# Message sums of the build stage moved from a VectorE addition to a ScalarE copy and an accumulating transfer

## The chip, the core and the metric

One core of one Trainium2 chip runs the whole program in one launch. The metric is the device time of the program in microseconds (us), lower is better. TensorE is written PE, VectorE DVE, ScalarE ACT, GpSimd POOL, and the queue of the sync engine SP, as in the profile.

## The reference, cut to what matters

Four graph layers run over the same 3125 nodes with 64 features and 103125 edges. The change lies in the first layer alone. It computes, for every edge (row, col), a similarity of the two transformed node vectors, and sums weighted vectors of the neighbours:

```python
Wh = h @ W + b
sim = sum(Wh[row] * Wh[col]) / max(|Wh[row]| * |Wh[col]|, EPS)
base = adj_v * softplus(deg_coeff[0] * deg_v + deg_coeff[1]) * (row != col)
prop_pos = segment_sum((base * relu(sim))[:, None] * Wh[col], row)
prop_neg = segment_sum((base * -relu(-sim))[:, None] * Wh[col], row)
out = scale * (coeff[0] * prop_pos + coeff[1] * prop_neg + coeff[2] * Wh)
```

## The kernel before

The nodes are cut into 25 blocks of 128 (`NB = 25`). The edges are sorted, and the stage `build` (L686 to L1244) turns them into dense blocks: for block b it makes the 128 by 3200 matrix of edge counts (`c_row`, bf16), of edge weights (`a_row`) and of gates (`g_row`). Counts and gates are stored to HBM for the later layers; the weights are used at once for the first layer. All five engines run their own program, tied by semaphores that count completed operations.

The work of one **step** (the function `step` of each engine, 24 of them, for blocks w = 1 to 24) is two things interleaved: the one-hot matmuls of block w, and the message passing of block v = w - 1.

- The one-hots: POOL doubles the edge fields of a quarter o of the slots (`double`, L780), DVE compares them with numbers and multiplies (`onehots`, L1008: the comparisons at L1018 and L1020, called "hi" and "soh" here, the product "mv" at L1024). PE multiplies them in 11 **lots** (`lot`, L1155); quarter 0 holds lots 0 to 2, quarter 1 lots 3 to 5, quarter 2 lots 6 to 8, quarter 3 lots 9 and 10. Lots use two pairs of PSUM banks in turn, so lot i waits until ACT has emptied lot i - 2. ACT empties a lot with three instructions (`evacuate`, L915, lines L927 twice and L931; lot 5 takes four).
- The messages: PE makes similarities of up to 1024 columns (`sims`, L1171), ACT takes their positive part (`positive`, L945, "pos"), DVE combines them ("sim", L1051). PE transposes the weights of four blocks into the one bank AT (`turn`, L1182), DVE multiplies them with the similarities ("y", L1062), PE multiplies y with the block's vectors (`propagate`, L1192, "prop"). There are seven chunks (turn, y and prop 0 to 6) and four groups g of them (sims, pos and sim 0 to 3; groups 0 to 2 have 1024 columns, group 3 has 128).
- The sums: for each group DVE adds the 128x512 result of two props to the tile `passed` in SBUF (`add`, L1070, the instruction at L1074; the fourth is 64x128). Props of groups 1 and 2 wait until the bank PR has been read by the add of the group before; turn 0 of the next block waits for the fourth add, which reads bank AT. The semaphore `added` counts the adds.

The order is written out by hand. PE and ACT both walk `ORDER` (L673), ACT acting only on its entries "sims" and "lot"; DVE walks `VORDER` (L677):

```python
ORDER = [("sims", 0), ("lot", 0), ("turn", 0), ("lot", 1), ("sims", 1), ("turn", 1), ("lot", 2), ("lot", 3), ("turn", 2),
         ("prop", 0), ("prop", 1), ("sims", 2), ("turn", 3), ("lot", 4), ("lot", 5), ("lot", 6), ("lot", 7), ("turn", 4),
         ("prop", 2), ("prop", 3), ("sims", 3), ("turn", 5), ("lot", 8), ("lot", 9), ("lot", 10), ("turn", 6), ("prop", 4),
         ("prop", 5), ("prop", 6)]
VORDER = [("sim", 0), ("y", 0), ("hi", 1), ("hot", 1), ("y", 1), ("sim", 1), ("y", 2), ("hi", 2), ("hot", 2), ("add", 0), ("y", 3),
          ("sim", 2), ("y", 4), ("hi", 3), ("hot", 3), ("add", 1), ("y", 5), ("hi", 0), ("sim", 3), ("y", 6),
          ("hot", 0), ("add", 2), ("add", 3)]
```

"hot" is soh and mv; index 0 of "hi" and "hot" belongs to the next block. POOL in a step copies two small weight tiles once the last prop of the block before is done (`weights`, L794, copies at L803 and L804), then doubles quarters 1, 2, 3 and quarter 0 of the next block. SP stores the gates of the block before in two pairs of transfers, after 4 and after 8 lots of the block have been emptied (`gated_out`, L875), and the counts when all are (`counts_out`, L870). ACT starts a step only once the stores from the tiles that it will overwrite have landed (`begin`, L935).

A second pass over the same code with a run-time index exists for graphs with nodes of very high degree. It does not run with these inputs.

Of the kernel before, what the change touches and what calls it, by code (L numbers as in the profile page):

```python
# [5 lines left out]
ALU = mybir.AluOpType  # L6
# [7 lines left out]
P = 128  # L14
N = 3125
F = 64
# [22 lines left out]
LOTS = [(o, a, min(a + LOT, OH[o][1])) for o in range(4) for a in range(OH[o][0], OH[o][1], LOT)]  # L39
HI = 26  # L40
SQ = 32
CHUNKS = [(a, min(4, NB - a)) for a in range(0, NB, 4)]
# [637 lines left out]


def rounds_of(eng, table):
    return eng.value_load(table[0:1, 0:1], min_val=1, max_val=-(-E // SLOTS) + 1)


def build(nc, k, table, st, st_dram, deg, rec_dram, whT, rn_row, cap, uD, coef, prop, c16_dram, c_dram, g_dram, prime_dram):  # L686
# [3 lines left out]
    with Mem(nc, "b") as l:  # L690
# [14 lines left out]
        begun = l.sb("begun", [P, 6])  # L705
        sim, scale = [l.sb(f"sim{i}", [P, 1024]) for i in range(2)], l.sb("scale", [P, 512])
        y = [l.sb(f"y{i}", [P, 1024]) for i in range(2)]
# [7 lines left out]
        s = {n: l.sem(n) for n in names.split()}  # L715
        s_win, s["further"] = k["win"], k["further"]
        s_stored = [l.sem(f"stored{i}") for i in range(2)]
# [39 lines left out]
        def _(pool):  # L757
# [48 lines left out]
            def add_out(r, b, par):  # L806
# [13 lines left out]
                pool.wait_ge(s["further"], done + 80)  # L820

            def first(r):
                weights(r, 0, 0)
                early = not again(r)
                double(r * NB, 0, 0)
                double(r * NB, 0, 1)
                if early:
                    gather(2, 5, 7)
                double(r * NB, 0, 2)
                if early:  # L830
                    gather(3, 7, 9)
                double(r * NB, 0, 3)
                if early:
                    gather(3, 9, 11)
                double(r * NB + 1, 1, 0)
                if early:
                    gather(4, 11, 13)
                    pool.wait_ge(s["rounded"], ROUNDED)

            def step(r, b, par):  # L840
                w = r * NB + b
                weights(r, b, par)
                if again(r):
                    add_out(r, b - 1, 1 - par)
                for o in range(1, 4):
                    double(w, b, o)
                if not (isinstance(b, int) and b == NB - 1):
                    double(w + 1, b + 1, 0)

            def widen():  # L850
# [46 lines left out]
        def _(act):  # L897
# [45 lines left out]
            def positive(v, g):  # L943
                act.wait_ge(s["sims"], NG * v + (NG + g + 1))
                nc.scalar.activation(side(pos, g), both(g), ACT.Relu, scale=coef[:, 0:1]).then_inc(s["pos"], 1)  # L945

            def first(r):
                w = r * NB
# [9 lines left out]
            def step(r, b, par):  # L958
                w = r * NB + b
                begin(r, w, b, par)  # L960
                for what, i in ORDER:
                    if what == "lot":
                        evacuate(r, w, par, i)
                    if what == "sims":
                        positive(w - 1, i)

            def end(r):
# [7 lines left out]
        def _(dve):  # L975
# [94 lines left out]
            def add(v, g):  # L1070
                m, n = (P, 512) if g < NG - 1 else (F, P)
                dve.wait_ge(s["propped"], NC * v + (2 * NC + 1 + min(2 * g + 2, NC)))
                part, bank = k["passed"][0:m, g, 0:n], PR if g < NG - 1 else AT
                nc.vector.tensor_tensor(part, part, ps[0:m, bank, 0:n], ALU.add).then_inc(s["added"], 1)  # L1074
# [783 lines left out]
def four_layers(nc, x, src, dst, edge_attr_16, edge_weight, edge_weight_n2, L0_gnn_W, L0_gnn_b, L0_gnn_deg_coeff,  # L1858
# [13 lines left out]
    with Mem(nc, "k") as top:  # L1872
# [5 lines left out]
        k["rows"], k["win"] = [top.sem(f"rows{g}") for g in range(len(GATES))], [top.sem(f"win{g}") for g in range(len(GROUPS))]  # L1878
        k["further"], k["starts"] = top.sem("further"), top.sem("starts")
        table = top.sb("table", [1, 2], I32)  # L1880
# [46 lines left out]
```

## Time and profile before

| | us |
|---|---|
| median of 3 runs | 1071.21 |
| lowest and highest run | 1067.58, 1077.04 |
| the profiled execution, its own time | 1065.46 |
| its span in the trace | 1063.8 |
| mean granted PE clock, share of full | 0.934 |

The stage `build` takes from about 99 us to about 706 us of the span; its 24 steps lie between 151 and 687 us. In the timeline a row is: start, duration, engine, line, operation, output tile <- input tiles, shapes, number of merged instructions, and in brackets how long the engine had been idle before it and who released it. Instructions of one engine overlap by about 0.1 us at their ends, so start-to-start distances are shorter than durations.

### The profile page before, as it was taken

The page shows a single profiled execution, that of the slowest core. Times are in us where ns is not written, and L with a number is a line of the kernel's source. Part 1 is how long each engine was busy: PE and PEld are TensorE (multiplying, and loading weights), DVE is VectorE, ACT ScalarE, POOL GpSimd, SP SyncE. Part 2 cuts the span into 40 slices and gives each one's busy share as a digit, 9 for nine tenths or more (in the row PEclk, how much of TensorE's full clock was granted, in tenths as well). Part 3 has the DMA queues.
Part 4 walks back from the last instruction along what each step waited for, and adds up shares of the span by engine and source line. Part 5 has one row for each costly group of instructions (what it writes and reads, how often), then busy time and mean ns, then how long its engine had stood idle before and what let it go on. Part 6 is the DMA issues. An engine that isn't in the chain of part 4 may idle for free. (4 is left out here: it accounts for less than half of the span.)

```text
span 1063.8 us, 33473 instructions
## 1 busy us (share of the span) xinstructions
PE 850.4 (80%) x14240; PEld 596.1 (56%) x14240; DVE 902.9 (85%) x1310; ACT 583.1 (55%) x1994; POOL 170.9 (16%) x316
## 2 busy tenths in 40 slices
PE   0596558877888878887878888755999998999997
PEld 0362435544455444554544545425999998996653
DVE  8977979999999999999999989856666798587896
ACT  0764546666676665666665756517999942112000
POOL 4814801121111211112211111100000000000000
PEclk9888669999999999999998989966999999997999
DMA  8933214543444434445334435549700000783893
GB/s 197 222 135 82 64 51 112 126 125 95 108 113 119 133 95 113 109 108 137 102 95 110 111 95 126 145 142 395 287 2 2 3 1 1 309 301 134 316 394 125
DMA packets 39321, 144.66 MB, mean 136 GB/s; under 512 B 13476, under 2 KB 14070, under 8 KB 35446
## 3 DMA queue, kind: packets, MB, share of 16 engines
q1 hardware_dynamic: 33990, 133.22, 42.3%
q0 software_dynamic: 2912, 7.92, 2.9%
q8 instruction: 117, 1.92, 0.7%
q10 hardware_dynamic: 2256, 1.23, 0.5%
q14 instruction: 46, 0.38, 0.1%
HBM read 78.63 MB, written 63.72 MB: 134 GB/s over the span
## 5 line engine op out<-in xcount | busy, mean ns | idle before, releaser
L1135 PE MATMUL b_ps<-b_mv,b_soh 64*128 64x50 bf16 (+1 forms) x9600 | 190.7, 190 | 111.1 <-DVE b_mv L1024 69.5
L1135 PEld LDWEIGHTS b_ps<-b_mv,b_soh 64*128 64x128 bf16 x9600 | 164.0, 95 | 161.6 <-DVE b_mv L1024 110.0
L1355 PE MATMUL layers_ps<-layers_u,layers_c 128*128 128x192 bf16 x2500 | 212.4, 248 | 11.8 <-ACT layers_u L1537 9.2
L1355 PEld LDWEIGHTS layers_ps<-layers_u,layers_c 128*128 128x128 bf16 x2500 | 209.4, 99 | 17.1 <-DVE layers_y L1661 8.0
L927 ACT ACTIVATE b_c_row<-b_ps 128x300 bf16<-128x300 f32 (+1 forms) x275 | 117.1, 426 | 83.9 <-PE b_ps L1135 78.7
L945 ACT ACTIVATE b_pos<-b_ps,k_coef 128x1024 f32<-128x1024 f32 x100 | 92.7, 927 | 125.4 <-PE b_ps L1135 118.5
L1024 DVE TENSOR_TENSOR b_mv<-b_mv,b_parts 128x2808 bf16<-128x2808 bf16 x100 | 147.9, 1479 | 0.0
L1062 DVE TENSOR_TENSOR b_y<-b_sim,b_ps 128x512 f32<-128x512 f32 (+1 forms) x175 | 109.7, 627 | 34.8 <-PE b_ps L1189 29.0
L1546 ACT ACTIVATE k_passed<-layers_c 128x128 bf16<-128x128 bf16 x450 | 131.4, 293 | 0.0
L1020 DVE TENSOR_TENSOR b_soh<-k_numbers,b_bits 128x2304 bf16<-128x2304 bf16 x100 | 121.9, 1219 | 0.0
L1135 PE MATMUL b_ps<-b_unit,b_wh_b 64*128 64x512 f32 (+1 forms) x350 | 102.5, 629 | 8.8 <-ACT b_fld L913 6.8
L1051 DVE SCALAR_TENSOR_TENSOR b_sim<-b_ps,k_coef,b_pos 128x1024 f32<-128x1024 f32 x100 | 104.1, 1041 | 5.8 <-ACT b_pos L945 5.8
L1135 PE MATMUL b_ps<-b_y,b_u_b 128*64 128x512 f32 (+1 forms) x350 | 93.2, 604 | 0.2 <-issue 0.2
L1694 DVE STREAM_TRANSPOSE layers_c<-layers_c 128x1600 f32<-128x1600 f32 x50 | 88.3, 1815 | 1.4 <-DMA layers_c<-g_blocks 0.8
L1546 ACT ACTIVATION_READ_ACCUMULATOR k_passed<-layers_c 128x1 f32 x450 | 84.0, 187 | 0.0
L1355 PE MATMUL layers_ps<-layers_c,layers_y 128*64 128x384 f32 (+1 forms) x400 | 74.1, 521 | 0.0
L1661 DVE TENSOR_REDUCE layers_y<-layers_ps 128x128 f32<-128x384 f32 (+1 forms) x52 | 28.1, 540 | 53.5 <-PE layers_ps L1355 53.3
L1135 PEld LDWEIGHTS b_ps<-b_unit,b_wh_b 64*128 64x128 f32 x350 | 31.8, 196 | 59.5 <-issue 33.9
L931 ACT ACTIVATE b_g_row<-b_ps 128x300 f32<-128x300 f32 (+1 forms) x156 | 63.7, 422 | 0.0
L792 POOL COPY b_bits<-b_fld 128x72 bf16<-128x72 bf16 x100 | 24.4, 244 | 239.0 <-DVE b_mv L1024 239.0
L1189 PE MATMUL b_ps<-k_ident,b_a_row 128*128 128x128 f32 x325 | 57.5, 296 | 4.9 <-DVE b_y L1062 2.6
L927 ACT ACTIVATE b_a_row<-b_ps 128x300 f32<-128x300 f32 (+1 forms) x143 | 61.2, 428 | 0.0
(272 smaller groups left out, 1065.6 us busy)
## 6 DMA issues: line engine op xcount, KB each, us to landing
layers_c<-g_blocks SPq DMA_DIRECT2D x25, 1600.0 KB, 9.0
g_blocks<-b_g_row SPq DMA_DIRECT2D x52, 400.0 KB
c_blocks<-b_c_row SPq DMA_DIRECT2D x25, 800.0 KB, 4.4
g_blocks<-head_odd SPq DMA_DIRECT2D x48, 400.0 KB, 4.3
layers_c<-c_blocks SPq DMA_DIRECT2D x12, 1600.0 KB, 26.9
prep_attr<-in_edge_attr SPq DMA_DIRECT2D x2, 1883.0 KB
prep_attr<-in_edge_attr SPq DMA_DIRECT2D x1, 1876.0 KB
rec<-sort_rec SPq DMA_DIRECT2D x1, 1209.0 KB, 4.5
```

Source lines behind the costliest of these rows:

```text
L927: nc.scalar.activation(out, src[:, :, at, :, :], ACT.Copy).then_inc(s["evac"], 1)
L931: ins = nc.scalar.activation(by_group[:, j, :, :, lo - SQ * j:hi - SQ * j], src[:, :, 2, :, lo - a:hi - a], ACT.Copy, scale=kept[:, 0:1] i ...
L945: nc.scalar.activation(side(pos, g), both(g), ACT.Relu, scale=coef[:, 0:1]).then_inc(s["pos"], 1)
L1020: nc.vector.tensor_tensor(halves(soh[b][:, 0:n, :]), nums(P), twice(1, P), ALU.is_equal)
L1024: nc.vector.tensor_tensor(mv[b][:, 0:n, 1:7, :].rearrange("p n q (h two) -> p n q h two", two=2), hi[:, :, None, :, :].to_broadcast(six), ...
L1051: nc.vector.scalar_tensor_tensor(side(sim[g % 2], g), both(g), coef[:, 1:2], side(pos, g), ALU.mult, ALU.add).then_inc(s["sgn"], 1)
L1062: nc.vector.tensor_tensor(y[g % 2][:, here], sim[g % 2][:, here], ps[:, AT, 0:n], ALU.mult).then_inc(s["scaled"], 1)
L1135: return nc.tensor.matmul(out, lhsT, rhs, start=start, stop=True, skip_group_check=True)
L1189: ins = nc.tensor.transpose(ps[:, AT, P * j:P * j + P], a_row[par][:, h0 + j, :], k["ident"][:])
L1355: return nc.tensor.matmul(out_, lhsT, rhs, start=start, stop=True, skip_group_check=True)
L1546: nc.scalar.activation(junk[:, at % 4, :], blocks[:, b, h * P:h * P + P], ACT.Copy, accum_out=counts[:, b, h:h + 1]).then_inc(s["counted"], 1)
L1694: v.transpose(gt[b % KEEP][:, i:i + 2, :, :].rearrange("p s h c -> p (s h c)"), rows[b % RING][:, i * SQ * NB:i * SQ * NB + n]).then_inc(s ...
```

## The change

For blocks 0 to 23 DVE no longer adds the messages to `passed`. ACT copies them from PSUM to a new SBUF tile `sent` (one buffer of 1664 columns), at four places of its order (`LEAVE`): group 0 after it has emptied lot 4, group 1 after lot 8, group 2 at prop 5, group 3 at prop 6. POOL then issues two accumulating transfers from `sent` into `passed`, 128 x 1536 and 64 x 128 numbers of fp32 (`message`), after its doublings of the step. ACT's first copy of a block waits for both transfers of the block before. POOL doubles quarter 1 one step earlier, at the end of the step before. The last block (24) keeps the four DVE adds, which now wait for the last transfer. The second pass is unchanged but for where its scratch tile lies.

```diff
+BYSUM = NB - 1
+LEAVE = [("lot", 4), ("lot", 8), ("prop", 5), ("prop", 6)]
...
+        sent = [l.sb(f"sent{i}", [P, 3 * 512 + P]) for i in range(1)]
+        sim, scale = [l.sb(f"sim{i}", [P, 1024]) for i in range(2)], sent[0][:, 0:512]
...
+            def message(v):
+                pool.wait_ge(s["added"], NG * v + NG + 1)
+                if v:
+                    pool.wait_ge(s["summed"], 32 * v)
+                pool.dma_start(k["passed"][:, 0:NG - 1, :].rearrange("p g n -> p (g n)"), sent[v % 1][:, 0:3 * 512],
+                               accum_op=ALU.add).then_inc(s["summed"], 16)
+                pool.dma_start(k["passed"][0:F, NG - 1, 0:P], sent[v % 1][0:F, 3 * 512:3 * 512 + P],
+                               accum_op=ALU.add).then_inc(s["summed"], 16)
...
 in POOL's first(r):
                 if early:
+                    double(1, 1, 1)
 in POOL's step(r, b, par):
-                for o in range(1, 4):
+                for o in range(2 if isinstance(w, int) else 1, 4):
                     double(w, b, o)
                 if not (isinstance(b, int) and b == NB - 1):
                     double(w + 1, b + 1, 0)
+                    if isinstance(w, int):
+                        double(w + 1, b + 1, 1)
+                if isinstance(w, int):
+                    message(b - 1)
...
+            def send(v, g):
+                m, n = (P, 512) if g < NG - 1 else (F, P)
+                act.wait_ge(s["propped"], NC * v + (2 * NC + 1 + min(2 * g + 2, NC)))
+                if v >= 1 and g == 0:
+                    act.wait_ge(s["summed"], 32 * (v - 0))
+                bank = PR if g < NG - 1 else AT
+                nc.scalar.activation(sent[v % 1][0:m, 512 * g:512 * g + n], ps[0:m, bank, 0:n], ACT.Copy).then_inc(s["added"], 1)
...
 in ACT's step(r, b, par), after what an entry of ORDER does:
+                    if isinstance(w, int) and w <= BYSUM:
+                        for g in range(NG):
+                            if (what, i) == LEAVE[g]:
+                                send(w - 1, g)
...
 in DVE's add(v, g):
+                if isinstance(v, int) and v < BYSUM:
+                    return
                 dve.wait_ge(s["propped"], NC * v + (2 * NC + 1 + min(2 * g + 2, NC)))
+                if isinstance(v, int) and v == BYSUM and g == 0:
+                    dve.wait_ge(s["summed"], 32 * BYSUM)
```

## Rows read from the trace of the kernel before

**Rows 1.** The page, busy time, share of the span and instructions of each engine.
```profile
PE 850.4 (80%) x14240; PEld 596.1 (56%) x14240; DVE 902.9 (85%) x1310; ACT 583.1 (55%) x1994; POOL 170.9 (16%) x316
```

**Rows 2.** Stretches of the span: busy us of each engine, granted clock, DMA share, GB/s.
```profile
core 0: us, PE busy (x) PEld busy (x) DVE busy (x) ACT busy (x) POOL busy (x), PEclk, DMA share, GB/s
350.00:400.00 50.00, 40.25 (x998) 25.51 (x998) 48.61 (x61) 33.62 (x88) 9.04 (x23) 1.00 0.41 101
...
550.00:600.00 50.00, 40.61 (x952) 24.24 (x950) 45.52 (x58) 31.13 (x80) 10.52 (x25) 0.93 0.44 112
```

**Rows 3.** Timeline, SP: issues of the counts' store, one a step (steps 1, 9, 10, 12, 13, 24).
```profile
168.15 0.34 SPq L870 DMA_DIRECT2D c_blocks<-b_c_row  x1
...
346.65 0.34 SPq L870 DMA_DIRECT2D c_blocks<-b_c_row  x1
...
368.51 0.34 SPq L870 DMA_DIRECT2D c_blocks<-b_c_row  x1
...
412.25 0.34 SPq L870 DMA_DIRECT2D c_blocks<-b_c_row  x1
...
435.70 0.34 SPq L870 DMA_DIRECT2D c_blocks<-b_c_row  x1
...
686.34 0.34 SPq L870 DMA_DIRECT2D c_blocks<-b_c_row  x1
```

**Rows 4.** Groups of instructions by shape, 150 to 687 us.
```profile
L1074 DVE TENSOR_TENSOR k_passed<-k_passed,b_ps 128x512 f32<-128x512 f32 x72 | 48.8, 677 | 0.7 <-PE b_ps L1135 0.7
L1074 DVE TENSOR_TENSOR k_passed<-k_passed,b_ps 64x128 f32<-64x128 f32 x23 | 6.2, 270 | 0.0
L945 ACT ACTIVATE b_pos<-b_ps,k_coef 128x1024 f32<-128x1024 f32 x71 | 79.1, 1114 | 85.0 <-PE b_ps L1135 78.0 <-DMA g_blocks<-b_g_row 3.5 <-DMA g_blocks<-head_odd 3.5
L945 ACT ACTIVATE b_pos<-b_ps,k_coef 128x128 f32<-128x128 f32 x24 | 8.8, 367 | 25.8 <-PE b_ps L1135 25.8
```

**Rows 5.** Timeline, around the boundary between steps 9 and 10.
```profile
345.97 0.29 DVE L1062 TENSOR_TENSOR b_y<-b_sim,b_ps 128x128 f32<-128x128 f32 x1 [0.31 <-PE b_ps L1189]
...
348.24 1.11 ACT L945 ACTIVATE b_pos<-b_ps,k_coef 128x1024 f32<-128x1024 f32 x1 [1.62 <-PE b_ps L1135]
349.07 0.87 DVE L1074 TENSOR_TENSOR k_passed<-k_passed,b_ps 128x512 f32<-128x512 f32 x2
...
349.87 1.27 DVE L1051 SCALAR_TENSOR_TENSOR b_sim<-b_ps,k_coef,b_pos 128x1024 f32<-128x1024 f32 x1
...
353.41 1.61 DVE L1024 TENSOR_TENSOR b_mv<-b_mv,b_parts 128x2808 bf16<-128x2808 bf16 x1
```

**Rows 6.** Timeline, from the first product mv of step 10 to its y 4.
```profile
358.50 1.11 ACT L945 ACTIVATE b_pos<-b_ps,k_coef 128x1024 f32<-128x1024 f32 x1 [1.60 <-PE b_ps L1135]
...
360.34 0.43 ACT L931 ACTIVATE b_g_row<-b_ps 128x300 f32<-128x300 f32 x1
...
360.64 0.44 ACT L927 ACTIVATE b_c_row<-b_ps 128x300 bf16<-128x300 f32 x1
...
361.82 0.71 PE L1135 MATMUL b_ps<-b_mv,b_soh 64*128 64x75 bf16 x36 [0.20 <-ACT b_g_row L931]
...
362.46 0.66 PE L1189 MATMUL b_ps<-k_ident,head_odd 128*128 128x128 f32 x4
...
363.25 0.69 DVE L1062 TENSOR_TENSOR b_y<-b_sim,b_ps 128x512 f32<-128x512 f32 x1 [0.16 <-PE b_ps L1189]
```

**Rows 7.** Timeline, the end of step 10.
```profile
367.37 0.33 PE L1189 MATMUL b_ps<-k_ident,head_odd 128*128 128x128 f32 x1
...
367.84 0.29 DVE L1062 TENSOR_TENSOR b_y<-b_sim,b_ps 128x128 f32<-128x128 f32 x1 [0.31 <-PE b_ps L1189]
```

**Rows 8.** DMA view, 343.5 to 369.5 us in 40 slices: busy tenths, and GB/s.
```profile
DMA  9999809891001000000001999999100079999943
GB/s 197 212 192 207 167 25 404 345 443 39 30 0 25 0 0 0 0 0 0 0 0 39 207 207 187 207 192 212 35 0 0 0 162 207 192 207 187 232 89 148
```

**Rows 9.** Timeline, POOL's indirect transfers beside DVE's one-hots, before the first step.
```profile
112.90 1.96 DVE L1024 TENSOR_TENSOR b_mv<-b_mv,b_parts 128x2808 bf16<-128x2808 bf16 x1
...
113.55 2.16 POOL L777 DMA_INDIRECT head_odd<-rec,head_idx  x1
...
122.58 0.95 POOL L777 DMA_INDIRECT head_odd<-rec,head_idx  x1 [0.31 <-issue]
```

**Rows 10.** Waits of 150 to 687 us: engine, line waited for: us in total, times, longest.
```profile
DVE b_y L1062 <- PE b_ps L1189: 25.0, 45, 1.8
```

More of the change, by code:

```diff
@@ L705, in build @@
         begun = l.sb("begun", [P, 6])
-        sim, scale = [l.sb(f"sim{i}", [P, 1024]) for i in range(2)], l.sb("scale", [P, 512])
+        sent = [l.sb(f"sent{i}", [P, 3 * 512 + P]) for i in range(1)]
+        sim, scale = [l.sb(f"sim{i}", [P, 1024]) for i in range(2)], sent[0][:, 0:512]
         y = [l.sb(f"y{i}", [P, 1024]) for i in range(2)]
@@ L715, in build @@
         s = {n: l.sem(n) for n in names.split()}
-        s_win, s["further"] = k["win"], k["further"]
+        s_win, s["further"], s["summed"] = k["win"], k["further"], k["summed"]
         s_stored = [l.sem(f"stored{i}") for i in range(2)]
@@ L1878, in four_layers @@
         k["rows"], k["win"] = [top.sem(f"rows{g}") for g in range(len(GATES))], [top.sem(f"win{g}") for g in range(len(GROUPS))]
-        k["further"], k["starts"] = top.sem("further"), top.sem("starts")
+        k["further"], k["starts"], k["summed"] = top.sem("further"), top.sem("starts"), top.sem("summed")
         table = top.sb("table", [1, 2], I32)
```

## The prediction

> **What bounds the kernel now.** I read the page first: DVE is the busiest engine, 85% of the span, PE 80%, ACT 55%, POOL 16% [rows 1]. The edit touches only the 24 steps of `build`, so next come stretches inside it: DVE is busy 48.61 us of 50 in a good stretch and 45.52 in a poor one, PE 40, ACT 31 to 34 [rows 2]. By occupancy DVE is the bound, and the additions sit on DVE. But 97% is not 100%, and there the argument turns: does another chain run as long as DVE's?
>
> The counts' store is issued once a step, which gives the length of a step: 346.65 to 368.51 is 21.86 us, a step without disturbance. From step 1 to step 24 it is (686.34 - 168.15) / 23 = 22.53 us on average [rows 3]; some steps are longer, as the one from 412.25 to 435.70, 23.45 us. So I take the regular step apart, in the timeline, by following who released whom. Four segments make the loop, and they add up to 21.87 us:
> - **A**, y 6 to sim 0: 345.97 to 349.87, 3.90 us. DVE does y 6, hot 0, add 2, add 3 without idling. The other way round to sim 0 goes y 6, prop 6, sims 0 on PE, pos 0 on ACT: it ends at 348.24 + 1.11 = 349.35 [rows 5].
> - **B**, sim 0 to the end of mv 1 (quarter 1): 349.87 to 353.41 + 1.61 = 355.02, 5.15 us, DVE without a gap [rows 5]. Nothing of the change is in it.
> - **C**, mv 1 to y 4: 355.02 to 363.25, 8.23 us. DVE has work nearly throughout, add 0 among it, but then y 4 waits 0.16 us for turn 4 on PE. That turn follows lot 7, and lot 7 waited 0.20 us until ACT had emptied lot 5; ACT ran without idling from pos 2 (358.50) on [rows 6]. So ACT and PE are the longer chain here, by 0.16 us.
> - **D**, y 4 to y 6: 363.25 to 367.84, 4.59 us. y 6 waits 0.31 us for turn 6 [rows 6, 7]. DVE, add 1 included, is again the shorter chain.
>
> These short waits of DVE for a turn come 45 times, 25.0 us in all [rows 10]: two a step, in nearly every step. In C and D an addition taken from DVE only makes the wait longer. That is the reading on which the forecast stands.
>
> **The change, part by part.**
>
> *The additions leave DVE.* Per block three of 0.677 us and one of 0.270 [rows 4], about 2.30 us; with the overlap of neighbours some 2.1 us less busy time, 24 x 2.1 = 50 us. What each is worth on the path:
> - add 2 and add 3 (A): 349.07 to 349.87, 0.80 us. Without them sim 0 waits for pos 0, which ends at 349.35; with about 0.1 us for the semaphore it starts at 349.46. Gain 0.41 us. The next operation, y 0, waits for turn 0, which ends just before the earlier sim 0 does, so the gain reaches B.
> - add 0 (C) and add 1 (D): nothing, as above. y 4 and y 6 wait some 0.6 us more each for PE.
>
> *The copies come to ACT.* No 128x512 copy from PSUM by ACT is in these rows; 128x128 takes 0.367 us and 128x1024 takes 1.114 [rows 4], those are the two ends. On a straight line 512 columns take 0.367 + 384 x 0.834 ns = 0.687 us. ACT's instructions overlap: 360.34 + 0.43 = 360.77, while the next begins at 360.64 [rows 6], so 0.11 to 0.13 us less. I take 0.58 us a copy (between 0.26 and 1.0), and 0.26 for the small one.
> - Copy 0 stands between the emptying of lot 4 and of lot 5. From 358.50 to lot 7 at 361.82 ACT has no slack, so lot 7, turn 4 and y 4 move by the full 0.58 us. This is the cost of the edit: C grows by 0.58 us.
> - Copy 1 stands behind lot 8. Lot 10 waits for the emptying of lot 8, which comes before the copy; prop 4 needs the copy, and turn 6 is ahead of it. I cost it at nothing; if lot 9's and 10's emptying became late, it would be up to 0.58.
> - Copies 1, 2 and 3 all stand before the next pos 0: 0.58 + 0.58 + 0.26 = 1.42 us. ACT idles 1.62 us there, waiting for sims 0 [rows 5]. They fit, with 0.2 us left. If they did not, segment A would lose its gain.
>
> *POOL.* Quarter 1's doubling is moved to the end of the step before; it waits for mv 3, which is then done, and takes its work out of the boundary. `message` waits for copy 3, some 0.2 us before pos 0, and behind it stand the two weight copies and the doubling of quarter 2, which DVE needs 8 us later. POOL is 16% busy; no one waits for it. A price remains: issuing an indirect transfer took POOL 0.95 to 2.16 us, and the mv beside the long one took 1.96 us where 1.61 is usual [rows 9, 5]. mv 0 of the next block stands exactly there: 0.35 us at most a step, and something back, since the weight copies no longer run beside it. I take 0.1 us (-0.1 to 0.35).
>
> *The transfers.* 128 x 1536 x 4 B = 786 KB a block. The trace has no accumulating transfer. They start about 1 us after copy 3, near 349 us on the clock of rows 5, and copy 0, by then 0.4 us earlier than its place at 360.64, needs them landed near 360.3. In that time the counts' store runs to about 350 us at 345 to 443 GB/s, then the engines are idle for 7 us, and from 357 the first pair of gate stores fills them at about 200 GB/s [rows 8]. With half the engines' time while another transfer runs, and 1 us kept for the landing, that leaves 0.6 + 6.8 + 1.2 = 8.6 us of engine time. At 400 GB/s the bytes take 2.0 us, at 200 GB/s 3.9; if reading the target as well doubles it, 7.9 at worst. So they should be just in time, and cost nothing. Were a transfer slower than 786 / 8.6 = 91 GB/s, copy 0 would wait, and each us more is a us on every step.
>
> The Trainium skill, in "Collectives: The Full Stack", section "The bandwidth ceiling: the fold count and why AG ≠ RS ≠ AR", says that a reducing transfer is half as fast as a copying one because it reads two sources, and not because adding costs time. By it the range of copy rates above would become 4 to 8 us, an estimate, and no stall would follow. No run here shows it yet.
>
> *The sum.* Per step: -0.41 (A) + 0.58 (C) + 0.1 (POOL beside DVE) = +0.27 us; times 24, +6.5 us. On the profiled execution: 1065.46 + 6.5 = 1072. That execution lies 5.75 us below the median of the runs, 1071.21; on the median the forecast is 1071.21 + 6.5, rounded to 1077 us. With copy 0 at 0.26 and POOL at -0.1 a step the sum is -0.25 x 24 = -6 us; with 1.0 and 0.35, +0.94 x 24 = +23 us: 1065 to 1094 for this case.
>
> **The rivals.**
>
> *R1, DVE's busy time decides.* If the chains through ACT and PE gave way, each step would lose the 2.1 us: 1071 - 50 = 1021 us. For it: 48.61 of 50 us busy [rows 2]. Against it: in 45 places DVE already waits for PE, and copy 0 makes that chain longer. A part of it, say copy 0 hidden by some slack that I don't see and only the 0.41 us kept, gives 1061 us. The Trainium skill, in "Perfetto Trace Analysis", section "Identifying the Most-Contended Engine", calls the engine with the highest occupancy the one to relieve; by that rule this rival would be the forecast, and the trace agrees with it only as to which engine is busiest. Chance 0.15, a third of it for the partial form.
>
> *R2, the accumulating transfer is late.* One mechanism, at ACT's wait for `summed` before copy 0. From copy 0 (360.3) to the end of copy 3 (near 369.9 on the same clock) are about 9.5 us and POOL's issue takes 1.2, so the step becomes 10.7 us plus the transfer's time from issue to landing, once that is over about 11.3 us; slower than before by 1% from 11.8. At 14 us each step is 24.7 us, + 2.8 x 24 = +68 us: 1139 us. At 12.5 us: +32 us, 1103. For it: only one buffer, a busy DMA at both ends of the window, an operation never seen here. Against it: 7 idle us in the middle [rows 8]. Chance 0.2, half of it above 1105.
>
> *R3, copies 1 to 3 make pos 0 late.* If they took 0.4 us more in all than I allow, A loses half its gain and the sum is about +0.5 x 24 = +12: 1083. Chance 0.15, a neighbour of the forecast.
>
> *R4, the change does nothing of note,* the two terms cancelling: 1071. That is within the forecast's range and counted with it.
>
> **How the numbers follow.** The forecast's own case has 0.5, R1 0.15, R2 0.2, R3 0.15. A measurement of this kernel can tell about 1% (10.7 us) from no change. Faster by over 1% (below 1060.5): R1 in its full form and a little of the partial one, 0.12. Slower by over 1% (above 1081.9): R2 without its mild part (0.17), half of R3, and a quarter of the forecast's case, 0.36. The rest, 0.52, is within 1%. The range reaches from 1060, leaving only the full R1 out (0.1), to 1105, leaving out the worse half of R2 (0.1); the likeliest case's own is 1065 to 1094.
>
> **What the profile of the changed kernel would show.** If I am right: the counts' stores of regular steps 22.0 to 22.3 us apart; DVE busy down to about 43 of 50 us in a stretch; the wait of y 4 grown from 0.16 to about 0.8 us and that of y 6 from 0.31 to about 0.9; lot 7's wait for ACT grown from 0.20 to about 0.8; an ACT copy of about 0.69 us, ending before pos 0 at the boundary; no ACT wait for a transfer before copy 0. The forecast is wrong if y 4 starts earlier after mv 1 than 8.23 us (then R1), if ACT's copy 0 is released by the software DMA queue (R2), or if pos 0 starts later than 1.25 us after sims 0 (R3).

## The result and the profile after

| | before | after |
|---|---|---|
| median of 10 runs, us | 1071.41 | 1064.70 |
| lowest and highest | 1067.58, 1077.04 | 1059.61, 1068.37 |
| the profiled execution, its own time | 1065.46 | 1059.61 |
| its span | 1063.8 | 1057.9 |
| mean granted clock | 0.934 | 0.943 |

The ratio is 0.9927, with an interval of 0.9899 to 0.9956: 0.7% faster, where 0.5% slower was forecast. It lies inside the range, but the sign was wrong. In the changed file DVE's y is L1093, sim L1082, mv L1055, the add L1109; PE's matmuls are L1170 and the turns L1224; ACT empties lots at L946 and L950, pos is L964, the new copy L972; POOL's transfers are L831 and L833; SP's counts' store is L889.

The page, busy time of each engine, and below it two stretches of the build stage (the columns are those of [rows 2]):
```profile
PE 840.5 (79%) x14240; PEld 593.2 (56%) x14240; DVE 854.9 (81%) x1214; ACT 619.2 (59%) x2090; POOL 175.8 (17%) x364
```
```profile
350.00:400.00 50.00, 40.42 (x996) 25.07 (x996) 44.08 (x52) 36.84 (x95) 11.32 (x30) 1.00 0.69 163
550.00:600.00 50.00, 39.61 (x994) 24.95 (x994) 43.38 (x51) 36.47 (x95) 10.18 (x29) 1.00 0.68 156
```
DVE lost 48 us of work over the program, the time only 7. DVE is now busy 44.08 of 50 us where it was 48.61 [rows 2], and the second stretch runs at clock 1.00 where it had 0.93. Hold on to that last number.

The issues of the counts' store, one a step (the first step, two neighbours in the middle, the last):
```profile
171.34 0.34 SPq L889 DMA_DIRECT2D c_blocks<-b_c_row  x1
...
350.23 0.34 SPq L889 DMA_DIRECT2D c_blocks<-b_c_row  x1
372.19 0.34 SPq L889 DMA_DIRECT2D c_blocks<-b_c_row  x1
...
681.05 0.34 SPq L889 DMA_DIRECT2D c_blocks<-b_c_row  x1
```
The regular step is 21.96 us; before it was 21.86 [rows 3]. So a step without disturbance is **longer** by 0.10 us, and still the 23 intervals together are shorter: 509.71 us against 518.19. The pieces of the span then are: up to the first store +3.2 us, the 23 intervals -8.5, all behind them -0.6, together -5.9. Taking the regular step 23 times away from each sum leaves what disturbed steps had on top: 15.4 us before, 4.6 after. So -8.5 is +2.3 from the regular step and -10.8 from the disturbed ones. The +3.2 us ahead of the first store lie in a part that the edit hardly touches, and this point moved between 165.4 and 174.4 us over the kernels of this study; I did not follow it.

**The regular step, segment by segment.** Timeline of the changed kernel, from y 6 of one step to y 4 of the next:
```profile
349.06 0.29 DVE L1093 TENSOR_TENSOR b_y<-b_sim,b_ps 128x128 f32<-128x128 f32 x1 [0.90 <-PE b_ps L1224]
...
350.00 0.78 ACT L972 ACTIVATE b_sent<-b_ps 128x512 f32<-128x512 f32 x2
...
351.08 0.88 POOL L831 DMA_DIRECT2D k_passed<-b_sent  x1 [3.46 <-ACT b_sent L972]
351.33 1.11 ACT L964 ACTIVATE b_pos<-b_ps,k_coef 128x1024 f32<-128x1024 f32 x1 [0.55 <-PE b_ps L1170]
...
352.55 1.28 DVE L1082 SCALAR_TENSOR_TENSOR b_sim<-b_ps,k_coef,b_pos 128x1024 f32<-128x1024 f32 x1 [0.40 <-ACT b_pos L964]
...
356.11 1.62 DVE L1055 TENSOR_TENSOR b_mv<-b_mv,b_parts 128x2808 bf16<-128x2808 bf16 x1
...
363.33 0.61 ACT L972 ACTIVATE b_sent<-b_ps 128x512 f32<-128x512 f32 x1
...
365.01 0.71 PE L1170 MATMUL b_ps<-b_mv,b_soh 64*128 64x75 bf16 x36 [0.69 <-ACT b_g_row L950]
...
366.44 0.69 DVE L1093 TENSOR_TENSOR b_y<-b_sim,b_ps 128x512 f32<-128x512 f32 x1 [1.23 <-PE b_ps L1224]
```
- A: 349.06 to 352.55 is 3.49 us, 0.41 less than 3.90. DVE now waits 0.40 us for pos 0, and pos 0 was not late: ACT still idled 0.55 us before it, where it had 1.62 [rows 5].
- B: 352.55 to 356.11 + 1.62 is 5.18 us; it was 5.15.
- C: 357.73 to 366.44 is 8.71 us, 0.48 more than 8.23. Copy 0 (363.33) pushes lot 7's wait for ACT from 0.20 to 0.69 us and y 4's wait from 0.16 to 1.23.
- D is the rest of the 21.96 us, 4.58; it was 4.59. y 6 waits 0.90 us where it had 0.31 [rows 7].

By group, 150 to 687 us, and DVE's waits of the same stretch (columns as in [rows 10]):
```profile
L972 ACT ACTIVATE b_sent<-b_ps 128x512 f32<-128x512 f32 x72 | 45.9, 638 | 0.0
L972 ACT ACTIVATE b_sent<-b_ps 64x128 f32<-64x128 f32 x24 | 6.7, 280 | 0.0
```
```profile
DVE b_y L1093 <- PE b_ps L1224: 55.9, 49, 2.5
...
DVE b_sim L1082 <- ACT b_pos L964: 16.6, 25, 4.2
```
The copy of 512 columns takes 0.638 us and costs the chain about 0.5. DVE's waits for turns doubled, from 25.0 [rows 10] to 55.9 us: an addition taken away there became idle time.

The transfers, from the page (last number: median us from issue to landing), and the one place where DVE waits for them, the first add of the last block:
```profile
k_passed<-b_sent POOLq DMA_DIRECT2D x24, 768.0 KB, 6.5
```
```profile
693.57 0.69 DVE L1109 TENSOR_TENSOR k_passed<-k_passed,b_ps 128x512 f32<-128x512 f32 x1 [3.11 <-DMA k_passed<-b_sent]
```
The large one lands after 6.5 us in the median (6.4 to 10.2), the small one behind it after 7.3 (up to 11.0); from the issue at 351.08 to copy 0 at 363.33 there are 12.2 us, and in no step did ACT wait for them. The last add's 3.11 us are partly paid: from the last counts' store to PE's first matmul on `passed` it is 705.82 - 681.05 = 24.8 us, where it was 709.16 - 686.34 = 22.8.

**The disturbed steps** come in two kinds. The first is a stall of PE, put down to "issue", with the clock at full. Lot 7 of the same step before, and then after:
```profile
272.02 0.68 PE L1135 MATMUL b_ps<-b_mv,b_soh 64*128 64x75 bf16 x34 [0.20 <-ACT b_g_row L931]
273.62 0.20 PE L1135 MATMUL b_ps<-b_mv,b_soh 64*128 64x50 bf16 x2 [0.92 <-issue]
```
```profile
276.06 0.68 PE L1170 MATMUL b_ps<-b_mv,b_soh 64*128 64x75 bf16 x34 [0.69 <-ACT b_g_row L950]
277.17 0.20 PE L1170 MATMUL b_ps<-b_mv,b_soh 64*128 64x50 bf16 x2 [0.43 <-issue]
```
0.20 + 0.92 before, 0.69 + 0.43 after: 1.12 us both times. What PE now waits for ACT, it no longer waits for "issue" behind it. Such stalls come in the same intervals of the 23: 3, 5, 7, 18 and 20 after, and before 3, 5, 7 and 20, where number 18 has a dip of the clock instead and shows its stall in the kernel of `early_doubling` below. Where no dip covers them they cost a step 1.1 to 1.25 us before and 0.5 to 0.8 after; I estimate about 3 us over the five.

The second kind is the clock. Slices of 1 us of the kernel before (PE busy first, granted clock third from the end), and PE there:
```profile
420.00:421.00 1.00, 0.32 (x20) 0.32 (x22) 1.00 (x2) 0.24 (x1) 0.31 (x2) 1.00 0.00 0
421.00:422.00 1.00, 1.00 (x32) 0.79 (x24) 1.00 (x2) 0.56 (x2) 0.14 (x1) 0.79 0.00 0
422.00:423.00 1.00, 1.00 (x4) 0.30 (x4) 0.91 (x2) 0.48 (x2) 0.00 (x0) 0.50 0.06 16
423.00:424.00 1.00, 1.00 (x4) 0.00 (x0) 1.00 (x3) 0.00 (x0) 0.00 (x0) 0.50 0.74 147
424.00:425.00 1.00, 1.00 (x4) 0.51 (x4) 1.00 (x2) 0.00 (x0) 0.00 (x0) 0.50 0.96 205
425.00:426.00 1.00, 1.00 (x8) 0.42 (x4) 1.00 (x1) 0.31 (x1) 0.00 (x0) 1.00 1.02 211
```
```profile
420.68 0.71 PE L1135 MATMUL b_ps<-b_mv,b_soh 64*128 64x75 bf16 x36 [1.53 <-DVE b_mv L1024]
...
422.17 1.97 PE L1135 MATMUL b_ps<-b_y,b_u_b 128*64 128x512 f32 x4
```
The clock falls to 0.50, which is 1.2 of the 2.4 GHz, about a us after the end of PE's wait of 1.53 us for mv, and it is back at 425. That wait doesn't tell why: it stands in every step, dip or not, with 1.53 us in nearly all of them before and 1.46 or 1.47 after. Props that take 1.08 us at full clock take 1.97, and the step takes 1.6 us more. The 15.4 us of before hold six steps with such a dip, one of them with a long one; the 4.6 us of after hold one. Where one dip follows another in the next step, they lie 23.9 us apart: before from 421.6 and 445.5 us on, and from 534.2, 558.1 and 582.0. A step with a dip lasts about as long, 23.5 us, so one dip may help to bring on the next; no run here tests that.

### The profile page after: what moved, and what is told of

It reads as the page before. It is cut to its first block and busy times, and to the rows that moved or that the text cites. A ratio compares the mean times of both kernels' runs of the same rounds, so it can differ in the third digit from the quotient of the medians.

```text
span 1057.9 us, 33568 instructions
## 1 busy us (share of the span) xinstructions
PE 840.5 (79%) x14240; PEld 593.2 (56%) x14240; DVE 854.9 (81%) x1214; ACT 619.2 (59%) x2090; POOL 175.8 (17%) x364
## 3 DMA queue, kind: packets, MB, share of 16 engines
q10 hardware_dynamic: 2256, 1.23, 0.5%
## 5 line engine op out<-in xcount | busy, mean ns | idle before, releaser
L1170 PE MATMUL b_ps<-b_mv,b_soh 64*128 64x50 bf16 (+1 forms) x9600 | 192.3, 189 | 119.9 <-DVE b_mv L1055 66.4
L1170 PEld LDWEIGHTS b_ps<-b_mv,b_soh 64*128 64x128 bf16 x9600 | 164.2, 95 | 171.9 <-DVE b_mv L1055 110.9
L946 ACT ACTIVATE b_c_row<-b_ps 128x300 bf16<-128x300 f32 (+1 forms) x275 | 119.7, 435 | 79.5 <-PE b_ps L1170 72.6
L1093 DVE TENSOR_TENSOR b_y<-b_sim,b_ps 128x512 f32<-128x512 f32 (+1 forms) x175 | 109.9, 628 | 63.9 <-PE b_ps L1224 59.3
L964 ACT ACTIVATE b_pos<-b_ps,k_coef 128x1024 f32<-128x1024 f32 x100 | 92.8, 928 | 91.9 <-PE b_ps L1170 90.7
L1055 DVE TENSOR_TENSOR b_mv<-b_mv,b_parts 128x2808 bf16<-128x2808 bf16 x100 | 145.6, 1456 | 0.0
L1082 DVE SCALAR_TENSOR_TENSOR b_sim<-b_ps,k_coef,b_pos 128x1024 f32<-128x1024 f32 x100 | 104.6, 1046 | 16.6 <-ACT b_pos L964 16.6
L1170 PE MATMUL b_ps<-b_unit,b_wh_b 64*128 64x512 f32 (+1 forms) x350 | 98.4, 605 | 8.9 <-ACT b_fld L932 6.8
L797 POOL COPY b_bits<-b_fld 128x72 bf16<-128x72 bf16 x100 | 39.2, 392 | 341.3 <-DVE b_mv L1055 341.3
L1170 PE MATMUL b_ps<-b_y,b_u_b 128*64 128x512 f32 (+1 forms) x350 | 88.4, 578 | 0.0
L950 ACT ACTIVATE b_g_row<-b_ps 128x300 f32<-128x300 f32 (+1 forms) x156 | 65.1, 432 | 0.0
L946 ACT ACTIVATE b_a_row<-b_ps 128x300 f32<-128x300 f32 (+1 forms) x143 | 62.8, 439 | 0.0
L1170 PEld LDWEIGHTS b_ps<-b_unit,b_wh_b 64*128 64x128 f32 x350 | 30.4, 188 | 55.8 <-issue 25.9
L1224 PE MATMUL b_ps<-k_ident,b_a_row 128*128 128x128 f32 x325 | 56.9, 293 | 5.2 <-DVE b_y L1093 4.8
```

Of the source, the lines that this page charges most:

```text
L946: nc.scalar.activation(out, src[:, :, at, :, :], ACT.Copy).then_inc(s["evac"], 1)
L950: ins = nc.scalar.activation(by_group[:, j, :, :, lo - SQ * j:hi - SQ * j], src[:, :, 2, :, lo - a:hi - a], ACT.Copy, scale=kept[:, 0:1] i ...
L1055: nc.vector.tensor_tensor(mv[b][:, 0:n, 1:7, :].rearrange("p n q (h two) -> p n q h two", two=2), hi[:, :, None, :, :].to_broadcast(six), ...
L1082: nc.vector.scalar_tensor_tensor(side(sim[g % 2], g), both(g), coef[:, 1:2], side(pos, g), ALU.mult, ALU.add).then_inc(s["sgn"], 1)
L1093: nc.vector.tensor_tensor(y[g % 2][:, here], sim[g % 2][:, here], ps[:, AT, 0:n], ALU.mult).then_inc(s["scaled"], 1)
L1170: return nc.tensor.matmul(out, lhsT, rhs, start=start, stop=True, skip_group_check=True)
```

## The experiments

Each kernel ran beside the kernel before on the same chip; ratios are to that. "Excess" is what the 23 intervals of a profile have over 23 regular steps.

**Is the difference real, and how much do the disturbed steps vary?** Both kernels were run again, unchanged.

> The kernel before, unchanged, profiled and timed once more, to see what repeats. Both theories expect regular steps of 21.86 us. Theory 1 (the change wins because fewer steps are stretched): the stretched steps come again, 8 to 11 of the 23 intervals, some 15 us in all, most of them beside a granted clock of 0.5 for 3.4 us, and the time of a run falls as its mean clock rises. Theory 2 (the first profile's dips were chance): another profile shows 2 or 3 dips or none.

> The changed kernel once more, unchanged. Theory 1 (its stretched steps are fewer and shorter for a reason: a stall of PE ahead of lot 7 is half hidden in lot 7's wait for ACT): regular steps of 21.96 us, stretched ones without a clock dip 0.5 to 0.7 us long in place of 1.1 to 1.25 before, all excess together 4 to 9 us; mean clock near 0.937 against 0.930. Theory 2 (chance): excess of 12 us or more, the clock as before.

Before again: ratio 0.9999 (0.997 to 1.0028), regular step 21.87, excess 16.1 us; ten of the 23 intervals are stretched, seven by dips, as theory 1 had it. After again: ratio 0.9949 (0.992 to 0.9978), regular step 21.96, excess 12.6 us, with six dips. This excess is what the theory of chance expected (12 us or more), not the 4 to 9 us of theory 1; the clock over the runs, 0.935 against 0.9265 of the kernel before on the same chip, is on the side of theory 1. The regular steps repeat to 0.01 us; the dips don't, so two profiles can't be compared by them, and the gain is rather half a per cent. Every run lists its clock, and that gives a mean over many: 84 runs of the kernel before, over all the chips used, have 0.9293 and 1070.7 us, the 22 of the kernel after 0.9355 and 1065.9. Within the runs of before, 0.001 of clock goes with 0.83 us, so the difference in clock, 0.0063, goes with 5.2 us: all of the 4.8 us between the means. At equal clock the two kernels take the same time, to within a us.

A run's mean clock doesn't say where in the program the clock was low. In the profile before it is 0.82 ahead of the first counts' store, 0.98 in the 23 intervals and 0.93 behind the last; after it is 0.80, 1.00 and 0.94. What speaks for the steps are the dips in the profiles: 6, 7 and 7 in the kernels of this study with DVE's additions and no added ACT work (before, before again, `early_doubling`), and 1, 6, 0, 2, 2, 2 and 3 in those without the additions (after, after again, `transfer_behind`, `no_transfer`, `copy_later`, `copy_later_padded`, `tiny_adds`).

**What are DVE's additions worth?** The kernel before, with the additions of blocks 0 to 23 cut to two columns:
```diff
                 dve.wait_ge(s["propped"], NC * v + (2 * NC + 1 + min(2 * g + 2, NC)))
+                if isinstance(v, int) and v < NB - 1:
+                    n = 2
```


> The kernel before, with the DVE adds of blocks 0 to 23 cut to 2 columns: the sums of those blocks are left out, no copies on ACT, no transfers. It prices the removal alone. Theory 1 (in segments C and D the chain through PE and ACT is as long as DVE's): the step falls by only 0.4 us, to about 21.4 to 21.5, the time by 10 us plus whatever stretched steps vanish. Rival (DVE's occupancy decides): the step falls by 1.5 to 2 us, the time by 35 to 50.

The ratio is 0.9793 (0.9754 to 0.9832), the regular step 21.47 us. Two steps of exactly that, 345.08 to 388.03 (columns as in [rows 2]):
```profile
345.08:388.03 42.95, 35.35 (x876) 22.03 (x874) 39.18 (x55) 28.85 (x76) 8.32 (x20) 1.00 0.48 117
```
and the same two steps in the kernel before:
```profile
346.65:390.37 43.72, 35.55 (x876) 22.16 (x874) 42.42 (x55) 29.00 (x76) 8.33 (x20) 1.00 0.47 115
```
DVE has 1.62 us less to do a step ((42.42 - 39.18) / 2), and the step gains 0.39. That is segment A's 0.41 and nothing else, as forecast; R1 would have given all of the 1.62. DVE was busy 97% and bounded only that part of the step. The rule of the Trainium skill that the prediction set against the trace ("Perfetto Trace Analysis", "Identifying the Most-Contended Engine") is not borne out here. The rest of the gain, some 13 us of 22, is no regular step: excess 12.0 us against 16.1, a clock of 0.945, and the rest behind or ahead of the steps.

**Is copy 0 what costs, and can it stand better?** Copy 0 behind the emptying of lot 5 instead of lot 4:
```diff
-LEAVE = [("lot", 4), ("lot", 8), ("prop", 5), ("prop", 6)]
+LEAVE = [("lot", 5), ("lot", 8), ("prop", 5), ("prop", 6)]
```


> ACT's copy of group 0 stands behind the emptying of lot 5 instead of lot 4. Theory 1 (copy 0 lies on the chain mv 1 - lot 3 - sims 2 - pos 2 - lot 4 - lot 5 - lot 7 - turn 4 - y 4, and cost it 0.5 us a step): the regular step falls from 21.97 to about 21.45 us, lot 7's wait for ACT from 0.69 back to about 0.2, y 4's wait from 1.23 to about 0.75, and the time by about 12 us against the changed kernel, 18 to 20 us against the kernel before. Rival (the place of copy 0 is of no account, a step is set elsewhere): within 3 us of the changed kernel.

The ratio is 0.9856 (0.9824 to 0.9887), 1054.08 us against 1069.67: better than the kernel before, and by the ratios better than the changed one; the 18 to 20 us expected against the kernel before are 15.6. The timeline of it shows why:
```profile
361.98 0.67 ACT L972 ACTIVATE b_sent<-b_ps 128x512 f32<-128x512 f32 x1
362.21 0.71 PE L1170 MATMUL b_ps<-b_mv,b_soh 64*128 64x75 bf16 x36 [0.20 <-ACT b_g_row L950]
...
363.64 0.69 DVE L1093 TENSOR_TENSOR b_y<-b_sim,b_ps 128x512 f32<-128x512 f32 x1 [0.75 <-PE b_ps L1224]
```
Lot 7 waits 0.20 us again, as before the change, and the copy runs beside it. The regular step is 21.47 us, the same as without the additions: copy 0 behind lot 4 cost 0.49 us a step, and behind lot 5 nothing. The stalls in the same steps are back at 1.0 to 1.5 us, since PE no longer waits ahead of them. The excess is 11.0 us.

**Do the transfers cost?** The changed kernel without them and without the waits for them:
```diff
-                if isinstance(w, int):
-                    message(b - 1)
...
-                if v >= 1 and g == 0:
-                    act.wait_ge(s["summed"], 32 * (v - 0))
...
-                if isinstance(v, int) and v == BYSUM and g == 0:
-                    dve.wait_ge(s["summed"], 32 * BYSUM)
```


> The changed kernel without POOL's accumulating transfers and the waits for them: the sums of blocks 0 to 23 are left out. Theory 1 (the transfer is in time, 6.5 us of a window of 11): regular steps of 21.9 to 22.0 as with it, the time within 3 us, but for some 2 us at the last add, which waited for the last transfer. Rival (the transfers cost by contention on POOL's port, on the DMA engines or on code loading): regular steps at least 0.1 us shorter, or fewer stretched ones, the time 3 us or more down.

The ratio is 0.9922 (0.9891 to 0.9954), the regular step 21.96 us, the excess 7.0. In the steps the transfers cost nothing. From the last counts' store to PE's first matmul on `passed` it is 22.3 us (701.38 - 679.13), 2.5 less than with them: that is the price of the last add's wait. The transfers do slow POOL itself: its copy of 128x72 in a doubling takes 0.46 us in the mean with them and 0.24 without, as in the kernel before, but no engine waited for it. And the large one twice, one after the other:
```diff
-                    pool.wait_ge(s["summed"], 32 * v)
+                    pool.wait_ge(s["summed"], 48 * v)
+                pool.dma_start(k["passed"][:, 0:NG - 1, :].rearrange("p g n -> p (g n)"), sent[v % 1][:, 0:3 * 512],
+                               accum_op=ALU.add).then_inc(s["summed"], 16)
+                pool.wait_ge(s["summed"], 48 * v + 16)
```
(ACT and the last block's add wait for the same sum of 48 a block instead of 32.)

> The changed kernel with the large accumulating transfer done twice, the second issued when the first has landed, so blocks 0 to 23 are counted twice; copy 0 waits for all of it. It prices a late transfer. By rival R2's formula: copy 0 to the end of copy 3 is 9.5 us, then two transfers of 6.5 us and up to 2 us of issue: a step of 24 to 25 us, + 48 to 70 us in all, ACT waiting for the software queue before copy 0. If instead the transfer had more room than 11 us, the step stays under 23.

The ratio is 1.1488 (1.1404 to 1.1571). The steps are about 31 and about 26 us long in turn. POOL, DVE and ACT in one of them:
```profile
383.44 0.86 POOL L834 DMA_DIRECT2D k_passed<-b_sent  x1 [7.16 <-DMA k_passed<-b_sent]
...
385.84 0.53 DVE L1052 TENSOR_TENSOR b_mv<-k_numbers,b_bits 128x468 bf16<-128x468 bf16 x1 [1.22 <-POOL b_bits L797]
...
394.93 0.60 ACT L975 ACTIVATE b_sent<-b_ps 128x512 f32<-128x512 f32 x1 [7.15 <-DMA k_passed<-b_sent]
```
ACT's copy 0 waits up to 10.0 us for the transfers, the wait that R2 names. The 24 to 25 us expected, 10.7 us plus two landings of 6.5, were missed: the steps have some 29 on average. Both terms came out larger. The first transfer was issued at 375.41, so it is 19.5 us to copy 0 at 394.93 and not 13; the medians to landing are 7.8 us for the first, 9.3 for the second and 9.9 for the small one behind it. And copy 0 to the end of copy 3 took 12.4 us in the block before (362.71 to 375.11), where 9.5 was taken. Two things go with it: the clock's mean is 0.858, and POOL, held 7.16 us by its own wait between the transfers, brings a doubling to DVE 1.22 us late. That second wait belongs to the test, and a single late transfer wouldn't have it, so the run doesn't price R2 as such.

**Does the half us of ACT cost half a us?** The kernel before with one more ACT instruction of 512 columns (SBUF to SBUF, used by no one) at copy 0's place:
```diff
                         evacuate(r, w, par, i)
+                        if i == 4 and isinstance(w, int):
+                            nc.scalar.activation(scale[:, :].rearrange("p (a n) -> p a n", a=4),
+                                                 k["ident"][:, None, :].to_broadcast([P, 4, P]), ACT.Copy)
```


> The kernel before, with nothing taken away, and one more ACT copy of 128x512 (from SBUF to SBUF, its result unused) behind the emptying of lot 4, where the change puts copy 0. It prices that copy alone. Theory 1: regular steps of 21.86 + 0.5 = 22.4 us, lot 7's wait for ACT 0.7; the stalls of PE ahead of lot 7 cost 0.5 to 0.7 us instead of 1.2, so the time grows by less than 12 us: by 5 to 10. Rival (ACT has slack at this place): steps of 21.9.

The ratio is 1.017 (1.0102 to 1.0238), +19.5 us. The 5 to 10 us were missed by far. Steps, and PE in one of them:
```profile
433.00 0.34 SPq L870 DMA_DIRECT2D c_blocks<-b_c_row  x1
...
456.90 0.34 SPq L870 DMA_DIRECT2D c_blocks<-b_c_row  x1
...
480.79 0.34 SPq L870 DMA_DIRECT2D c_blocks<-b_c_row  x1
```
```profile
443.18 1.98 PE L1138 MATMUL b_ps<-b_y,b_u_b 128*64 128x512 f32 x4
...
450.20 0.71 PE L1138 MATMUL b_ps<-b_mv,b_soh 64*128 64x75 bf16 x36 [0.71 <-ACT head_odd L931]
```
The wait of lot 7 is 0.71 us, as expected, so the undisturbed step would be some 22.4 us. But nearly every step is 23.9 us, and 22 of the 23 have a dip of the clock, at the same place, as the props of 1.98 us show; the one without it, with a stall, has 23.00 us. Two more kernels go the same way. Copy 0 of the changed kernel done twice:
```diff
+                if g == 0:
+                    nc.scalar.activation(sent[v % 1][0:m, 512:512 + n], ps[0:m, bank, 0:n], ACT.Copy)
```


> The changed kernel, with copy 0 done twice on ACT (the first into a part of the tile that copy 1 overwrites). Theory 1: copy 0 lies on the chain with its whole length, so regular steps grow by another 0.5, to 22.5 us, and the time by 10 to 12 us over the changed kernel. Rival (segment C has slack left): below 22.2.

And with a copy of 128 columns ahead of it:
```diff
+                if g == 0:
+                    nc.scalar.activation(sent[v % 1][0:m, 512:640], ps[0:m, bank, 0:128], ACT.Copy)
```


> The changed kernel with a further ACT copy of only 128x128 before copy 0 (0.26 us more on the chain). Runs so far: steps of 21.5 us had 2 to 4 clock dips of 3.4 us in 23 steps, 21.9 and 22.0 had 1 to 8, and where the undisturbed step would be 22.4 or 22.5 one dip came in every step, 23.9 us after the last, and made the step 23.90. If the dips depend on the length of the step: undisturbed steps of 22.2 us, between 8 dips and one in every step, mean clock below 0.925, the time 10 to 35 us over the changed kernel. If the copies of copy_alone and copy_twice brought the dips in another way: few dips as in the changed kernel, and about 6 us more.

Ratios 1.0339 (1.0284 to 1.0394) and 1.0274 (1.0212 to 1.0336). With the copy done twice all steps have a dip and nearly all are 23.9 us, and the mean clock is 0.905; the 10 to 12 us expected over the changed kernel are 40 on the same chip. With the quarter the first two intervals are 22.14 and 22.13 us, 0.18 more than the changed kernel's, which is the copy's price in the step (it takes 0.29 us itself); the other 21 are 23.7 to 24.4, and the time is by the ratios 37 to 39 us over the changed kernel, beyond the 10 to 35 expected. So a copy that lengthens the undisturbed step by less than 0.2 us took a kernel with rarer dips to one that has them in nearly every step.

**What made the dips rarer?** Three tries, each for one part of the change. The earlier doubling of quarter 1, alone, in the kernel before:
```diff
                 if early:
+                    double(1, 1, 1)
...
-                for o in range(1, 4):
+                for o in range(2 if isinstance(w, int) else 1, 4):
...
+                    if isinstance(w, int):
+                        double(w + 1, b + 1, 1)
```


> The kernel before, with only the change's move of quarter 1's doubling to the end of the step before. If POOL's part carries some of the gain (mv 0 runs beside fewer POOL copies): mv 0 nearer 1.61 us than 1.71, and fewer clock dips than the 7 and 8 of the kernel before. If not: regular steps of 21.86 us, as many dips, the time within 3 us of the kernel before.

Ratio 0.9995 (0.9949 to 1.0041), step 21.86, excess 16.1 us: it is not this. POOL's weight copies ahead of the transfers, so that mv 0 has its old neighbours (at the end of a step, `message(b - 1)` goes; it stands behind the next step's `weights` instead, the last one at POOL's end):
```diff
                 weights(r, b, par)
+                if isinstance(w, int) and b >= 2:
+                    message(b - 2)
...
-                if isinstance(w, int):
-                    message(b - 1)
```


> The changed kernel with POOL's two weight copies put ahead of the transfers again, as in the kernel before, so that they run beside mv 0 and the transfers start some 2 us later. What is asked is why the changed kernel has fewer clock dips though its undisturbed step is 0.1 us longer. If mv 0 (1.71 us beside the weight copies, 1.62 without) and the shorter idle time of PE behind it are the cause: mv 0 back to 1.71 us, the step 22.0 to 22.1 us, 6 or more dips, mean clock 0.931 or below, the time that of the kernel before or over it. If they are not: mv 0 at 1.71 us, but clock and time as in the changed kernel, 0.993 to 0.996 of before. The transfer, 6.5 us in a window of 11, is still in time in both cases.

Ratio 0.9959 (0.9935 to 0.9983), step 21.97, excess 3.3 us, with no dip in the steps; the mean of all large mv is 1.645 us again (1.643 before, 1.615 after). The gain stays, so it is not POOL's order. And the better kernel (copy 0 behind lot 5) with its step lengthened again, by an ACT copy of 288 columns behind lot 4:
```diff
+                    if isinstance(w, int) and (what, i) == ("lot", 4):
+                        act.wait_ge(s["propped"], NC * (w - 1) + (2 * NC + 3))
+                        if w > 1:
+                            act.wait_ge(s["summed"], 32 * (w - 1))
+                        nc.scalar.activation(sent[0][:, 512:800], ps[:, PR, 0:288], ACT.Copy)
```


> The kernel of copy_later (undisturbed step 21.47 us) with an ACT copy of 128x288, result unused, behind the emptying of lot 4: 0.39 us on the chain, so that its undisturbed step has the length of the kernel before, 21.86 us, while DVE still has no additions. Asked: is the step's length alone what sets the number of clock dips? If it is: mean clock 0.927 to 0.932 as before, 7 or 8 dips, the time 0.995 to 1.0 of before. If DVE's missing additions (or what they do to PE's waits) also count: clock 0.935 or more, fewer dips, the time 0.992 or less of before.

Ratio 0.9945 (0.992 to 0.9971), step 21.78 us, excess 9.6 us. Its mean clock is 0.9362 beside 0.9296 of the kernel before on the same chip, though its step is nearly as long as that one's 21.86; its ratio lies between the two expectations (0.995 to 1.0, and 0.992 or less). The changed kernel says the same more plainly: its step is longer than the one before, its clock higher. So the length of the step alone doesn't set how often the dips come. What all kernels with the higher clock share is that DVE has no, or hardly any, additions; but `copy_twice` and `copy_and_quarter` have none either, and a dip in nearly every step. PE's wait for mv 1 doesn't decide it alone: it is 1.53 us where DVE has the additions and 1.37 to 1.47 in most steps where it hasn't, but 1.47 in `copy_and_quarter` too. The cause stays open.

## Why the prediction was wrong, point by point

- **The reading of the bound (C and D bounded by PE and ACT, A by DVE): right.** Taking the additions away (tiny_adds) gave 0.39 us a step, forecast 0.41 for A and nothing for C and D.
- **A, -0.41: right** (3.90 to 3.49 us). R3 did not come: ACT still idled 0.55 us before pos 0. Its sign was set too close: pos 0 started 1.26 us after sims 0, a hair beyond the 1.25 named, which is what it was before.
- **Copy 0, +0.58 a step in C: right in kind, 0.1 too large.** The straight line gave 0.687 us for the copy, it took 0.638; C grew by 0.48 us. Moving the copy away gave 0.49 back. Lot 7's wait, forecast 0.8, is 0.69; y 4's, forecast 0.8, is 1.23: the prediction's own parts, 0.16 + 0.58 + 0.6, already make 1.3. y 6's, forecast 0.9, is 0.90.
- **POOL beside DVE, +0.1: wrong in size.** B grew by 0.03 us, and the first product of the new step, forecast to suffer beside the transfers' issue, takes 1.62 us where it took 1.71 before, beside the weight copies.
- **The transfers: right in the steps.** 6.5 us to landing, no wait of ACT in any step, no change of the step without them. Missed was the one wait outside the steps, the last block's add, at some 2 us. The rule of the Trainium skill in "Collectives: The Full Stack", section "The bandwidth ceiling: the fold count and why AG ≠ RS ≠ AR", would have put them at 4 to 8 us, an estimate. The landing agrees with that without showing it: no run here copies the same bytes without adding.
- **Per step +0.27: it was +0.10.** With that alone the sum would have been +2.4 us instead of +6.5, and still slower. (1071.21 + 6.5 rounds to 1078, not 1077; nothing hangs on it.)
- **The step that failed** is "some steps are longer ... so I take the regular step apart", together with "times 24". It carried the 15 us of the disturbed steps over unchanged, as if they had nothing to do with the edit. They did. The stalls behind lot 7 shrank by what PE now waits there for ACT, about -3 us. And the clock was low for less time: over all runs its mean is 0.0063 higher, which goes with 5 us. Against these stand +2.3 us of the regular step and the last add's 2 us. Together that is about -4 us, where 5 to 7 us were measured; the terms come from different sets of runs, and the last 1 to 3 us are not accounted for.
- **R1** is refuted in its full form; the forecast's sign came out as in its partial form (1061 us), for another reason. **R2** was not reached; the forced case has steps of 29 us and not 24, but with longer landings and a wait of POOL that R2 doesn't have. **R4**, the two terms cancelling, was nearest to the truth of the regular step.

That fewer dips are the gain rests on the clocks of 106 runs and ten profiles, not on an edit that changes the dips alone; why this kernel has fewer, three experiments did not settle.

## What to carry to other kernels

In a pipeline with a fixed period, a sum over the regular step is only good to the size of the disturbed steps. List all periods of the profile, give each long one its cause, and ask what the edit does to these too before forecasting less than a per cent. Put work that is added to a chained engine behind the instruction that another engine waits for, not ahead of it: one place later in the same order was worth 0.49 us a step, and made the change twice as good.

## What was not expected of the hardware

- A dip of the granted clock to 0.50 adds 1.6 us to a step of these two kernels, and 1.5 to 2.0 in the others. Whether it comes seldom or in every step can hang on 0.2 us of step length: 22.14 us steps turned to 23.7 and more.
- A stall put down to "issue" is absorbed by a wait that happens to lie ahead of it (0.20 + 0.92 and 0.69 + 0.43 us).
- The accumulating transfer within SBUF moved 768 KB in 6.5 us from issue to landing in the median, at 0.88 us of POOL. PE, ACT and DVE kept their pace beside it; POOL's own copies behind it took 0.46 us instead of 0.24.
